# Query tiles of a latent self-attention: full 128-row tiles for two sequences instead of one padded head each

## The reference

```
Wdkv   = x @ latent_w + latent_b                      # (b, t, 72), keys and values of all heads
q      = einsum('btc,hcl->bhtl', x, Wd_w) + Wd_b      # (b, 16, t, 72)
scores = einsum('bhtl,bsl->bhts', q, Wdkv) / sqrt(d_head)
attn   = softmax(where(causal, scores, -inf))
y      = einsum('bhts,bsl->bhtl', attn, Wdkv)
out    = transpose(y).reshape(b, t, 16 * 72) @ out_w + out_b
x      = layernorm(x + out)
```

## Time and profile before

| | |
|---|---|
| median of 3 runs | 3462.93 us (3460.24 to 3462.98) |
| span of the profiled execution | 3459.8 us |
| TensorE busy | 3335.2 us, 96% |
| VectorE, ScalarE, GpSimd busy | 2465.0, 2327.3, 1405.8 us |
| mean granted TensorE clock | 0.983 |
| DMA, mean | 49 GB/s |

### The profile page before, as it was taken

One profiled execution on the slowest core, in us unless ns is written; L12 is line 12 of the kernel. 1 busy time (PEld: TensorE's weight loads), 2 busy tenths in 40 slices (PEclk: granted clock), 3 DMA queues, 4 the chain that ended last, 5 costly groups with the idle time before them and its releaser, 6 DMA issues. The chain is left out here.

```text
span 3459.8 us, 87103 instructions
## 1 busy us (share of the span) xinstructions
PE 3335.2 (96%) x25744; PEld 3202.2 (93%) x25744; DVE 2465.0 (71%) x7109; ACT 2327.3 (67%) x7480; POOL 1405.8 (41%) x2905
## 2 busy tenths in 40 slices
PE   7999999999999997999999999999589999989999
PEld 7999999999999996999999999999578888879999
DVE  6878888888888886677777777777744545437777
ACT  6888888888888885777777777777534444434443
POOL 4656666666665664333333333333432323200000
PEclk9999999999999998999999999999789999999999
DMA  2000000000000001010101010010223333314443
GB/s 104 17 20 19 28 19 19 19 19 19 19 19 19 21 24 64 17 31 21 33 21 30 24 30 27 24 33 15 70 73 116 97 115 97 115 52 121 122 122 100
DMA packets 150252, 169.25 MB, mean 49 GB/s; under 512 B 19488, under 2 KB 135072, under 8 KB 149664
## 3 DMA queue, kind: packets, MB, share of 16 engines
q1 hardware_dynamic: 143904, 150.53, 14.2%
q0 software_dynamic: 6144, 16.79, 1.6%
HBM read 125.33 MB, written 41.94 MB: 48 GB/s over the span
## 5 line engine op out<-in xcount | busy, mean ns | idle before, releaser
L702 POOL TENSOR_SCALAR ca_prob<-ca_prob,ca_inverse 128x120 f32<-128x120 f32 x1024 | 354.6, 365 | 646.7 <-DVE ca_inverse L967 644.6
L466 ACT ACTIVATE sa_prob<-sa_prob,sa_shift 128x128 f32<-128x128 f32 (+1 forms) x1024 | 453.7, 461 | 2.8 <-DVE sa_shift L520 2.8
L910 ACT ACTIVATE ca_prob<-bank,ca_shift 128x120 f32<-128x120 f32 x1024 | 355.1, 369 | 0.1
L434 ACT ACTIVATE sa_q_hi<-bank,sa_qbias 128x256 fp32r<-128x256 f32 x512 | 214.4, 470 | 205.9 <-PE bank L111 205.9
L535 DVE SCALAR_TENSOR_TENSOR sa_q_lo<-bank,sa_qbias,sa_q_hi 96x256 fp32r<-96x256 f32 x512 | 219.8, 469 | 176.1 <-ACT sa_q_hi L434 176.1
L289 POOL TENSOR_SCALAR sa_prob<-sa_prob,sa_inverse 128x128 f32<-128x128 f32 x512 | 190.6, 372 | 376.6 <-DVE sa_inverse L528 361.7
L520 DVE CUSTOM_DVE_ANT_0 sa_prob<-bank,sa_mask 128x128 f32<-128x128 f32 (+1 forms) x1024 | 303.9, 350 | 0.0
L1249 POOL DMA_INDIRECT ex_x_raw<-mid_x,ex_tokens x128 | 160.8, 1256 | 346.3 <-PE bank L1265 312.6
L109 PE MATMUL bank<-sa_xT_hi,sa_wd_hi 128*128 128x256 f32 x1024 | 289.0, 282 | 12.6 <-DVE sa_wd_lo L483 11.2
L110 PE MATMUL bank<-sa_xT_lo,sa_wd_hi 128*128 128x256 f32 x1024 | 287.3, 281 | 0.0
L111 PE MATMUL bank<-sa_xT_hi,sa_wd_lo 128*128 128x256 f32 x1024 | 287.0, 280 | 0.0
(11 more groups left out here) (249 smaller groups left out, 12943.5 us busy)
## 6 DMA issues: line engine op xcount, KB each, us to landing
mid_eo<-ex_out SPq DMA_DIRECT2D x32, 512.0 KB, 2.9
co_eo_raw<-mid_eo SPq DMA_DIRECT2D x128, 128.0 KB, 2.6
sa_xT_raw<-in_xT SPq DMA_DIRECT2D x32, 256.0 KB, 3.6
sa_x_res<-in_x SPq DMA_DIRECT2D x32, 256.0 KB, 3.0
mid_x<-sa_x SPq DMA_DIRECT2D x32, 256.0 KB, 3.0
ca_x_raw<-mid_x SPq DMA_DIRECT2D x32, 256.0 KB, 2.8
ca_x_res<-mid_x SPq DMA_DIRECT2D x32, 256.0 KB, 2.7
mid_x<-ca_x SPq DMA_DIRECT2D x32, 256.0 KB, 2.1
```

The source lines that it names most:

```text
L466: act.activation(prob[:, r, hh, cols], prob[:, r, hh, cols], ACT.Exp, bias=shift[:, r, n:n + 1], scale=-1.0, accum_out=total[:, r, n:n + 1 ...
L702: ins = pool.tensor_scalar(prob[:, r, t, hh], prob[:, r, t, hh], inverse[:, r, n:n + 1], 1.0, ALU.mult, ALU.mult)
L910: act.activation(prob[:, r, t, hh], SC[g % 2][:, n * S:n * S + S], ACT.Exp, bias=shift[:, r, n:n + 1], accum_out=total[:, r, n:n + 1]).the ...
```

## The change

Queries are made for two sequences at once. `x` of both lies side by side, so one matmul has 512 columns, and the 16 x 72 = 1152 query rows are made as nine tiles of 128 rows with no padding. A tile holds pieces of two or three heads. ScalarE and VectorE write its high and low part to `q_tile` (two buffers), and SyncE moves each piece to its head's rows in `q`, with the repeated rows, by copies from SBUF to SBUF (semaphores q_in). GpSimd's copy L298 is gone. Pairs of heads of the two sequences alternate: slot g is sequence g % 2. Sixteen slots make a group of two sequences; the nine tiles are made in the slots Q_SLOT, the keys of both sequences in slot 0 and their transposes in slot 1, now in the PSUM bank of the queries. Scores of the first 128 tokens take only the first 128 keys. The output product has a bank for each sequence. `pT` has two buffers instead of four. Some of the diff:

```diff
-        QL, SL, IL, TL, PL, OL = 1, 3, 4, 5, 7, 9
-        KV_MM, KV_TR, RES, NORM = 2, 4, 12, 17
+        KV_MM, KV_TR = 0, 1
+        Q_SLOT = (2, 3, 5, 6, 8, 9, 11, 13, 14)
+        X_NEXT, X_SPLIT = 3, 15
+        SL, IL, TL, PL, OL = 6, 7, 8, 10, 12
+        LAST = GROUP - 2
+        RES_IN, RES, NORM = 12, GROUP + 4, LAST + OL + 1
...
@@ SyncE
+                    t = tile_at(m)
+                    if t is not None and group_exists(J, c):
+                        j = t % QT
+                        need_alone(sp, qlo_done, upto_tile(J, t), spare_sp)
+                        need(sp, s_mm, upto_slot(J, c * GROUP + 2 * (pieces(j)[-1][0] // 2 - RING) + 1, 2))
+                        for h, lo, end, row in pieces(j):
+                            n, r, hh = end - lo, h // 2 % RING, h % 2
+                            sp.dma_start(f32(q[lo:end, r, hh]), f32(q_tile[row:row + n, t % 2])).then_inc(q_in[t % 2], 16)
+                            if end > REST:
+                                at = max(lo, REST)
+                                sp.dma_start(f32(q[L + at - REST:L + end - REST, r, hh, 0]),
+                                             f32(q_tile[row + at - lo:row + n, t % 2, 0])).then_inc(q_in[t % 2], 16)
+                            if lo < REST:
+                                to = min(end, REST)
+                                sp.dma_start(f32(q[AT + lo:AT + to, r, hh, 1]), f32(q_tile[row:row + to - lo, t % 2, 0])).then_inc(q_in[t % 2], 16)
...
@@ TensorE
+                        if i == 0:
+                            for t in (c * QT + p, c * QT + p + 1):
+                                need(pe, q_in[t % 2], moved(J, t))
                         for hh in range(2):
-                            need(pe, s_read, upto(J, g - 1, 4, 2 * hh - 2))
+                            need(pe, s_read, upto_slot(J, g - 1, 4, 2 * hh - 2))
                             for t in range(TT):
-                                mm = two(pe, SC[hh][:, t * T:t * T + T], q_hi[:, r, hh, tk], q_lo[:, r, hh, tk],
-                                         kvT_a[:, b], kvT_b[:, b], True, True)
+                                mm = two(pe, SC[hh][:, t * T:t * T + (t + 1) * P], q[:, r, hh, 0, i, tk], q[:, r, hh, 1, i, tk],
+                                         kvT_a[:, k, i, keys], kvT_b[:, k, i, keys], True, True)
...
-                        for hh in range(2):
-                            w = slice((2 * p + hh) * P, (2 * p + hh + 1) * P)
-                            for k in range(KC):
-                                mm = three(pe, Q[:, hh * T:hh * T + T], wd_hi[:, k, w], wd_lo[:, k, w],
-                                           x_hi[:, b, k], x_lo[:, b, k], k == 0, k == KC - 1)
+                        for k in range(KC):
+                            mm = three(pe, Q[:], wd_hi[:, k, w], wd_lo[:, k, w], x_hi[:, k], x_lo[:, k], k == 0, k == KC - 1)
```

More of the change, by code:

```diff
@@ L144, in f32, with upto_slot, upto_group, upto_row @@
     return ap.bitcast(F32)
+QT = H * L // P
+SA_BODY = 32
+SA_BODIES = B * NP // SA_BODY
+SA_GROUPS = SA_BODY // (2 * NP)
+GROUP = 2 * NP
+GROUPS = B // 2
+def upto_slot(J, g, per=1, more=0):
+    return J * (SA_BODY * per) + (per * (g + 1) + more)
+def upto_group(J, c, per=1, more=0):
+    return J * (SA_GROUPS * per) + (per * (c + 1) + more)
+def upto_row(J, c, i, per=1, more=0):
+    return J * (2 * SA_GROUPS * per) + (per * (2 * c + i + 1) + more)
+def upto_tile(J, t, per=1, more=0):
+    return J * (SA_GROUPS * QT * per) + (per * (t + 1) + more)
+def slot_exists(J, g):
+    return not isinstance(J, int) or 0 <= SA_BODY * J + g < B * NP
+def group_exists(J, c):
+    return not isinstance(J, int) or 0 <= SA_GROUPS * J + c < GROUPS
+def pieces(j):
+    out, row = [], j * P
+    while row < (j + 1) * P:
+        h, first = row // L, row % L
+        end = min(L, first + (j + 1) * P - row)
+        out.append((h, first, end, row - j * P))
+        row += end - first
+    return out
+def moves(piece):
+    _, first, end, _ = piece
+    return 1 + (end > REST) + (first < REST)
+TILE_MOVES = [sum(moves(piece) for piece in pieces(j)) for j in range(QT)]
+def moved(J, t):
+    later, t = divmod(t, SA_GROUPS * QT)
+    own = [n for k, n in enumerate(TILE_MOVES * SA_GROUPS) if k % 2 == t % 2]
+    return J * (16 * sum(own)) + 16 * (later * sum(own) + sum(own[:t // 2 + 1]))
 def self_attention(nc, bank, ident, wv_raw, wv_in, d):
@@ L326, in body @@
+                    c, u = m // GROUP, m % GROUP
+                    if u == KV_MM and group_exists(J, c):
+                        need(pe, xlo_done, upto_group(J, c))
+                        need(pe, qlo_done, upto_tile(J, c * QT - 1))
                         for k in range(KC):
-                            mm = three(pe, KV[:, 0:T], lw_hi[:, k], lw_lo[:, k], x_hi[:, b % 2, k], x_lo[:, b % 2, k],
-                                       k == 0, k == KC - 1)
+                            mm = three(pe, Q[:], lw_hi[:, k], lw_lo[:, k], x_hi[:, k], x_lo[:, k], k == 0, k == KC - 1)
@@ L363, in body @@
                         out = PV[:].rearrange("l (h t) -> l h t", h=2)
-                        three(pe, out, kv_hi[:, b, 0], kv_lo[:, b, 0], pT_hi[:, r, :, 0:T], pT_lo[:, r, :, 0:T], True, False)
-                        three(pe, out[:, :, P:T], kv_hi[:, b, 1], kv_lo[:, b, 1], pT_hi[:, r, :, T:3 * P],
+                        three(pe, out, kv_hi[:, k, i, 0], kv_lo[:, k, i, 0], pT_hi[:, r, :, 0:T], pT_lo[:, r, :, 0:T], True, False)
+                        three(pe, out[:, :, P:T], kv_hi[:, k, i, 1], kv_lo[:, k, i, 1], pT_hi[:, r, :, T:3 * P],
@@ L392, in body @@
                                 tk = slice(t * P, t * P + P)
[L394 removed]
+                                mm = two(pe, O[i][:, t * C:t * C + C], y_hi[:, r, hh, tk], y_lo[:, r, hh, tk], ow[:, 0, w],
                                          ow[:, 1, w], p == 0 and hh == 0 and t == 0, p == NP - 1 and hh == 1)
                         mm.then_inc(o_mm, 1)
[L398 removed]
+            over_bodies(pe, body, 1, SA_BODIES, SA_BODIES + 1)
         @block.scalar
```

431 lines of the change are left out of this document (217 added, 214 removed).

## The result

The changed kernel takes **3431.14 us** (median of four runs, 3427.26 to 3436.78) against 3462.95 for the kernel before on the same chip: a ratio of 0.9909, 95% interval 0.9895 to 0.9923. It is 0.9% faster, which is clear of the runs' noise, in the range that was given, and 31 us short of the 3400 us forecast. The profiled execution has a span of 3435.1 us, against 3459.8.

The account below looks back on a forecast made before the run. TensorE, without a gap in mid self-attention, was taken as the bound. Span: 3459.8 - 173 saved + 107 given back in stalls + 3 for fill and drain = 3397 us, so median 3400 us; range 3305 to 3445 us.

Parts of the forecast that it names:

- TensorE's saving: In self-attention, fewer query matmuls and shorter scores save TensorE 5.4 us a sequence, 173 us over 32.
- Scores at 0.11 us: In self-attention, score matmuls cut to 128 columns take 0.11 us each, saving 0.3 us per sequence.
- Waits at slots 13, 14, 0, 1 and 2: In self-attention, other engines' order makes TensorE wait 1.65, 1.25, 1.2, 1.45 and 0.3 us: 5.9 us per two sequences.
- What a stall costs besides: In self-attention, each of about eight stalls exposes a weight load, 0.1 us each: 0.8 us per two sequences.
- Copies hidden: In self-attention, tile-to-head copies stay hidden: 63 issues at 0.51 us take 32 of 78 us, with 2 us to spare.
- the 0.8 that was named as a sign of being wrong: In self-attention, SyncE's issues spaced over 0.8 us would show the forecast wrong.
- Fill and drain: At self-attention's ends, a deeper pipe and first copies queued behind weight loads cost +3 us (-10 to +15).
- Later stages are the same code: nothing: Stages after self-attention keep their code, so their time was taken to change by nothing.
- gap-free: Rival, 14%: TensorE stays without gaps in self-attention; 3293 us, with small stalls up to 3330.
- late copies: Rival, 14%: SBUF copies land in 6 to 7 us instead of 3.6, adding 30 to 50 us; 3430 to 3455.
- SyncE: Rival, 7%: SyncE's queue of copy issues becomes the bound in self-attention; slower, 3590 us at 1.3 us per issue.
- the shorter matmuls: Rival, 5%: self-attention's 128-column score matmuls take 0.08 us, saving another 31 us; 3369 us.

Follow-up runs that it names:

- e8_values_early: The changed kernel with three VectorE operations late, self-attention's loop written out, and the values' transposes, kv_hi and kv_lo moved earlier in slot 1; 3307.46 us.
- e10_full_keys: As e8_values_early, but with the first 128 queries' scores again over all 256 keys; 3314.92 us.
- e1 to e3: Three runs, each moving one VectorE operation later in the changed kernel: x1, the keys' corrections, x_lo; 3398.72, 3410.98 and 3418.52 us.
- e5_unrolled: As e4_all_late, with self-attention's loop written out as straight code on every engine; 3326.88 us.
- e6_before_pairs: The kernel before with its self-attention loop made twice as long, two bodies of 16 steps a turn, nothing reordered; 3474.86 us.
- e4_all_late: The changed kernel with x1, the keys' corrections and x_lo all moved later on VectorE together; 3371.84 us.
- e11_only_unrolled: The changed kernel with its self-attention loop written out and nothing else; 3404.5 us.

## Why the prediction held, and where it was short

- **TensorE's saving** was right in its parts. A short slot takes 3.60 us (3.59 forecast), a slot with a query tile 4.99 (4.97), the group without a wait 71.9 (71.6; e8_values_early). The sum, however, used 5.4 us x 32 = 173, where the prediction's own slots give 16 x (82.06 - 71.6) = 167; measured groups (82.27 and 71.94) give 165. Those 6 us were never there.
- **Scores at 0.11 us**: right as a sum, by 0.93 us for eight and by e10_full_keys. Of the rule of 81 ns, in the Trainium skill "TensorE: Matmul & The Clock Gate" (Back-to-back issue gap), nothing is won here: the two short matmuls start their successors after 0.06 and 0.11 us, 85 ns on average, but the two of 256 columns behind them then take 0.145 each instead of 0.12, and the four took 0.46 us together.
- **Waits at slots 13, 14, 0, 1 and 2**: forecast 1.65, 1.25, 1.2, 1.45 and 0.3 us, measured 1.29, 0.53 (0.37 before the scores, 0.16 before the tile), 1.54, 1.53 and 0.09. Their sum is 5.0 against 5.9. The causes of the first four are shown by e1 to e3, each of which removes its own, but for the part of slot 0 that is the loop's: its mean is two things, 0.9 us within a turn of the loop and 1.9 to 2.7 at its turning back.
- **What a stall costs besides**: 0.8 us a group was put down for weight loads laid bare. The group is 79.5, and 71.9 + 5.0 leaves 2.6. The scores right behind these waits, at full clock, take 1.10 and 1.22 us in slots 0 and 1, 1.01 in 2, 1.12 and 1.28 in 13 and 14 instead of 0.93: 1.1 us together, near the 0.8. The rest is the slow clock: 11 stretches of 3.4 to 6.8 us, 48 us in all at half the clock in self-attention, so up to 24 us lost, 1.5 a group. The prediction had no term for it. A whole group was forecast at 78.3 and takes 79.5; at both ends of self-attention, where slots have no tile to make, the changed kernel gets some of it back. Between the output products 173 - 107 = 66 us were forecast and 51.7 came: 6 of the missing 14 are the sum's, 8 these waits' and the clock's.
- **Copies hidden**: right. In e5_unrolled and e8_values_early no wait on a copy is left in steady state. SyncE's issues of them took 0.71 us each (mean of those between 200 and 1200 us) and stood 0.75 from start to start, not 0.51: 63 x 0.75 = 47 us of 79.5 were still enough, and the queue is farther from free than was said, near the 0.8 that was named as a sign of being wrong.
- **Fill and drain**: 10.1 us, not 3. TensorE stands 15.2 us in two waits that the trace puts down to the first tiles' copies:

```profile
32.19 0.56 SPq L339 DMA_DIRECT2D sa_q<-sa_q_tile  x1
35.28 0.45 PE L116 MATMUL bank<-sa_kvT_a,sa_q 128*128 128x128 f32 x1 [9.15 <-DMA sa_q<-sa_q_tile]
...
44.19 2.35 DVE L675 SCALAR_TENSOR_TENSOR sa_ow<-sa_ow,sa_minus_low,sa_ow_raw 128x2048 fp32r<-128x2048 f32 x1 [2.79 <-ACT sa_ow L568]
46.46 0.28 DVE L626 CUSTOM_DVE_ANT_0 sa_prob<-bank,sa_mask 128x128 f32<-128x128 f32 x1
...
47.25 0.45 PE L116 MATMUL bank<-sa_kvT_a,sa_q 128*128 128x128 f32 x1 [6.04 <-DMA sa_q<-sa_q_tile]
```

The first scores need two tiles. SyncE issued the first tile's six copies from 21.2 to 25.8 us, then two loads of x, then the second tile's eight from 27.1 to 32.75 (the first line): the first wait is mostly these issues, one after the other. The prediction had put 3 us on fill and drain together, with the first copies behind the weights' loads, and no price on the issues there. The second wait is no copy's: the copies of the first three tiles had moved all their packets by 39.5 us. TensorE started when VectorE had read the scores before, and that reading stood behind VectorE's correction of the output weights, which had waited 2.79 us for ScalarE. Both are read from the rows and not tested.

- **"Later stages are the same code: nothing"** is the step that failed. It is the largest term: 17.1 us. The code was the same, and the place of the program was not.

Together: 6 + 8 + 7 + 17 = 38 us, which is 3435.1 less the 3396.8 us that the sum gave for the span; by the medians 31 are missing. The range held the result because it was wide, and because waits forecast too long (5.9 for 5.0 us a group) stood in for a part of the clock that had no term; that is luck and no merit of the terms put at nothing. Of the rivals, gap-free came true only after five changes more; late copies, SyncE and the shorter matmuls were wrong.

What the stops are is argued, not shown. That a turn of a long loop fetches its instructions anew fits three things. The first is the length: in the traces a turn of self-attention has 1473 instructions of TensorE (matmuls, weight loads and its sequencer's) in the kernel before, which does not stop, 2351 in the changed kernel and 2906 in e6_before_pairs, which do; for ScalarE it is 380 and 716, for VectorE 363 and 677 (in e6_before_pairs 748 and 715, where a stop of theirs would be hidden behind TensorE's). The second is that straight code has no stops. The third is cross-attention, where the packets of q14 come and go with ScalarE's stops in all fourteen kernels: 6 to 9 in each 100 us where the stage takes 1067 to 1070 us, none where it takes 1052. In self-attention the packets alone tell less. q8 lost 15 of its 104 packets when TensorE's loop was written out, and q14 none, so q8 carries TensorE's; between 200 and 1200 us it has one packet in the kernel before and 5 to 8 in each 100 us of the changed kernel, but with the loop written out it still has 5 or 6, and TensorE never stops. q14 has 10 to 16 in the kernel before, more than the changed kernel's 6 to 12. So fetching as such does not stop an engine; that it stops one where the loop turns back is the part that was not tested. Why an offset of 275 helps and 64 does not was not tried further.

## What to carry to other kernels

Where an engine's order puts an operation that waits for another engine ahead of the one that the bounding engine needs, move it behind; the price can be read off by laying out one slot from the rows, as was done here to within 0.4 us for four of five places (the mean of slot 0, 1.54 for 1.2, is close in part by luck: 0.9 by the chain and the rest by the loop). Count a longer loop body as a change of its own: look for stops at the turns, one per turn, that the trace puts down to "issue" or to a transfer long done. Do not take the releaser that the trace names for the cause; check what else the instruction waited for, as with the second wait of the fill. And compare the stages whose code did not change, with a look at the instruction queues: a stage can move by 1.6% without an edit in it.

## What the runs showed of the hardware

- At the turning back of a loop of 32 slots, TensorE stopped for 2.9 to 3.8 us, ScalarE and VectorE for up to 3.6 and 3.7; with 32 steps in the kernel before, TensorE for 1.7 on average. With 16 steps TensorE had none.
- ScalarE's loop in cross-attention stopped for 1.9 to 2.5 us in each turn or not at all, by its place in the program.
- Behind waits of TensorE the granted clock often fell to 1.2 GHz for 3.4 or 6.8 us, while TensorE was already busy again: five times behind the six stops of 2.9 to 3.8 us in e4_all_late, and nine times in e11_only_unrolled, where no wait is over 1.5 us but four slots of a group have one. With one wait of 1.4 us in a group (e5_unrolled) it did not fall.
- A 128-column matmul gains little beside weight loads of 128 columns, which started 0.11 to 0.12 us apart: half of the columns saved 0.008 us per matmul.
